# A graph convolution with a mixture of experts on one core: odd experts walk their chunks downwards, and the scaling stage is laid out anew

## The chip, the cores and the metric

The kernel runs on one core of a Trainium2 chip. The metric is the device time of one execution in microseconds (us). Engines are named as in the profile: PE is TensorE (PEld its weight loads), DVE is VectorE, ACT is ScalarE, POOL is GpSimd, SP is SyncE, which here only issues DMAs. L680 is line 680 of the kernel before.

## The reference

The input is `x` (12500 nodes of 256 features), 200000 edges `src`, `dst` (sorted by `dst`), a memory row `r`, and the weights of eight experts. Cut to what matters:

```python
h    = layernorm(x);  mems = h with row y replaced by r
near = the 7 rows of mems nearest to r          # squared distance
deg  = number of edges into a node (+7 for y) + 2;  dinv = 1 / sqrt(deg)
out[c] = sum over edges (s -> c) of dinv[s]*dinv[c]*(mems @ W)[s]  +  2*dinv[c]^2 * (mems @ W)[c]
x    = x + out
h    = layernorm(x)
e    = argmax(softmax(h @ gate_w + gate_b));  p = its probability
pos  = rank of the token among those of its expert; kept = pos < 1954
x    = x + p * kept * (relu(h @ w1[e] + b1[e]) @ w2[e] + b2[e])
```

## The kernel before

**Stage 1, to about 217 us.** The nodes lie in SBUF as 98 windows of 128 nodes (`nodes`), in seven chunks of 14 windows. POOL gathers 98 rows of sorted edges, one indirect DMA for each window (L665), in batches of seven; ACT counts in them (`count_first`, L761), which gives the degrees. Behind the count of each batch, ACT does ten squares (`far_square`, L766) of differences to `r` that DVE forms (`far_rows`, L1079, with `r_rows` in SBUF; a ring of 16 windows). When the degrees are known, each window is scaled in place by dinv and the layer norm: `scale_chunk`, chunks 1 and 6 on ACT (L772), the other five on DVE (L1208). SP stores each scaled chunk, in order from 0 to 6, into `z_table` in HBM (L535). ACT then clears `counts_f`, 6272 words in each partition (L794). PE turns the windows and ACT and DVE write them back as the start of the aggregate (L800, L1221).

**Stage 2, to about 1790 us.** POOL issues 1216 gathers of 128 rows from `z_table` (L680), after it has waited for the stores of all seven chunks. PE multiplies them with one-hot matrices (L1818), four gathers to a group; DVE adds the groups up. The ring holds four groups. Other edges are counted in `counts_f` and multiplied with pieces of `z_table` that SP loads. Convolution, second layer norm and gating run in the shadow of this. At the end `list_i` holds for each expert and place the row to fetch, and `taken_i` how many tokens each expert has.

**Stage 3, to the end.** An expert has room for 1954 tokens, eight chunks of 256 (`CHUNKS`, the last with 162). The 64 chunks are numbered n = 0 to 63, and s = n modulo 16 inside a pair of experts. All engines walk over all chunks, and a branch on the number of tokens taken skips the work on a chunk that starts beyond it; the semaphores of a skipped chunk are still counted up. PE does `up` (L2059), the transposes of the next chunk's rows (`turn_chunk`, L2041) and `down` (L2071). DVE copies the transposed rows (`feats`, L1638) and forms the results (`results`, L1670 to L1690). ACT normalizes the fetched rows of every chunk, skipped or not (`norm_rows`, L913), and does the bias and relu (L943).

POOL has no branch: it fetches and writes every chunk, skipped ones too (rows of a skipped chunk are written out of bounds, and so dropped).

```python
for n in range(FETCH):                 # FETCH = 6
    fetch(n)                           # two indirect DMAs, L729
for n in range(NE * NCH):
    if n + FETCH < NE * NCH:
        fetch(n + FETCH)
    for t in range(2):
        pool.wait_ge(S["res_ok"], 2 * n + t + 3)
        ... indirect DMA to out, L740
    if n % PC == PC - 1:               # the end of a pair of experts
        ... wait for the writes; sem_inc(S["pair_sent"], 1)
```

SP loads the weights of expert e + 2 (2 MB, L540, L541) when the results of expert e are through or skipped; there are two sets of weights.

Of the kernel before, what the change touches and what calls it, by code (L numbers as in the profile page):

```python
# [10 lines left out]
P = 128  # L11


def build(nc, x, src, dst, gnn_r, gnn_w, yidx, gate_w, gate_b, w1, b1, w2, b2, out):
# [79 lines left out]
    Z_ACT = (1, 6)  # L94
    Z_DVE = [c for c in range(NZC) if c not in Z_ACT]
    SQ_EACH, SQ_MID = 10, 4
    FAR_TO = [16, 30, 46, 60, 76, NW]
# [83 lines left out]
    PC = 2 * NCH  # L181
    XSLOTS = 8
    FB2 = FT // 2
    assert PC % XSLOTS == 0 and NCH % 2 == 0 and FB2 == 4 and KD == 2
# [3 lines left out]
    with ctx:  # L188
# [18 lines left out]
        count_up = bank[7][:, 0:P]  # L207
        strip_bank = [bank[2], bank[3]]
# [412 lines left out]
        def _(pool):  # L621
# [47 lines left out]

            for c in range(NZC):  # L670
                pool.wait_ge(chunk_moved[c], STORED[c])
# [49 lines left out]
            def fetch(n):  # L721

                slot = n % XSLOTS
                if n >= XSLOTS:
                    pool.wait_ge(S["res_ok"], 2 * (n - XSLOTS) + 4)
                    pool.wait_ge(S["xh_ok"], 2 * (n - XSLOTS) + 2)
                for t in range(2):
                    rows = list_i[:, 2 * n + t:2 * n + t + 1]
                    nc.gpsimd.indirect_dma_start(xs_rows[:, slot, t, :], None, x_rows,  # L729
                                                 bass.IndirectOffsetOnAxis(ap=rows, axis=0)).then_inc(S[f"xs_in{slot}"], 16)  # L730
# [3 lines left out]
            for n in range(NE * NCH):  # L734
                if n + FETCH < NE * NCH:
                    fetch(n + FETCH)
                for t in range(2):
                    m, slot = min(P, CHUNKS[n % NCH][1] - t * P), n % 2 * 2 + t
                    pool.wait_ge(S["res_ok"], 2 * n + t + 3)
                    nc.gpsimd.indirect_dma_start(  # L740
                        out, bass.IndirectOffsetOnAxis(ap=out_idx[0:m, 2 * n + t:2 * n + t + 1], axis=0), o_tile[0:m, slot, :], None,
                        bounds_check=last_node, oob_is_err=False).then_inc(S[f"out_done{slot}"], 16)
                if n % PC == PC - 1:
                    for slot in range(4):
                        pool.wait_ge(S[f"out_done{slot}"], 16 * (n + 1) // 2)
                    pool.sem_inc(S["pair_sent"], 1)
# [3 lines left out]
        def _(act):  # L750
# [40 lines left out]
            scale_chunk(Z_ACT[1])  # L791

            act.wait_ge(S["less_ok"], NW)
            nc.scalar.activation(counts_f, zeros[:, 0:1].to_broadcast([P, P * NW // 2]), ACT.Copy).then_inc(S["counts_clear"], 1)  # L794
# [128 lines left out]
            for q in range(NE // 2):  # L923
# [7 lines left out]
                for j in range(2):  # L931
                    for c in range(NCH):
                        n, s = CHUNKS[c][1], j * NCH + c
# [5 lines left out]
                        with act.If(all_took[q * 2 + j] > CHUNKS[c][0]):  # L939
                            act.wait_ge(S["l2_ps"], q * (2 * PC) + (2 * s + 2))  # L940
                            for f in range(FT):
                                act.wait_ge(S["l1_ps"], q * (PC * FB2) + ((s + 2) * FB2 + f // 2 + 1))
                                nc.scalar.activation(hid[:, f, 0:n], up_bank[f // 2][:, f % 2 * CR:f % 2 * CR + n], ACT.Relu,  # L943
                                                     bias=b1_pair[:, j * FT + f:j * FT + f + 1]).then_inc(S["hid_ok"], 1)
# [6 lines left out]
        def _(dve):  # L951
# [122 lines left out]
            def far_rows(first, last):  # L1074

                for w in range(first, last):
                    if w >= FR:
                        dve.wait_ge(S["square_ok"], w - FR + 1)
                    nc.vector.scalar_tensor_tensor(diff[:, w % FR, :, :], nodes[:, :, w, :], rstd[:, w:w + 1],  # L1079
                                                   r_rows[:, :].rearrange("p (k c) -> p k c", k=KD),  # L1080
                                                   ALU.mult, ALU.subtract).then_inc(S["diff_ok"], 1)
# [59 lines left out]

            far_rows(0, FAR_TO[0])
# [69 lines left out]
            for c in Z_DVE:  # L1212
                if c == Z_DVE[-1]:
                    far_rows(FAR_TO[4], FAR_TO[5])
                scale_chunk(c)

# [44 lines left out]

            dve.wait_ge(S["count_up_ps"], 1)
# [369 lines left out]
            def feats(q, s, took):  # L1632

                n = CHUNKS[s % NCH][1]
                with dve.If(took > CHUNKS[s % NCH][0]):
# [18 lines left out]
            def results(q, s, took):  # L1654

                j, c = s // NCH, s % NCH
                with dve.If(took > CHUNKS[c][0]):
                    for t in range(2):
                        n, slot = min(P, CHUNKS[c][1] - t * P), s % 2 * 2 + t
# [62 lines left out]
        def _(pe):  # L1722
# [28 lines left out]
            pe.wait_ge(S["row_id"], 3)  # L1751
            nc.tensor.matmul(count_up, ident[:, :], iota_r[:, :], start=True, stop=True).then_inc(S["count_up_ps"], 1)
# [280 lines left out]
            def turn_chunk(q, s):  # L2033

                n = CHUNKS[s % NCH][1]
# [13 lines left out]
            def up(q, s):  # L2049
                j, n = s // NCH, CHUNKS[s % NCH][1]  # L2050
                pe.wait_ge(S["xT_ok"], q * PC + (s + 3))
                if s % NCH == 0:
# [10 lines left out]
            def down(q, s):  # L2063
                j, n = s // NCH, CHUNKS[s % NCH][1]
# [16 lines left out]
            def turn_or_skip(q, s, took):  # L2081
                with pe.If(took > CHUNKS[s % NCH][0]):
# [5 lines left out]
            for q in range(NE // 2):  # L2088
                took = all_took[2 * q:2 * q + 3]
                for s in range(PC):  # L2090
                    inside = s % NCH < NCH - 1
                    with pe.If(took[s // NCH] > CHUNKS[s % NCH][0]):
# [4 lines left out]
                    with pe.Else():  # L2097
# [3 lines left out]
                        if inside:  # L2101
                            skip_turn(q, s + 1)
                    if not inside:
# [23 lines left out]
```

## Time and profile before

| | |
|---|---|
| median of 3 runs | 2517.27 us (2515.47 to 2517.34) |
| profiled execution | 2514.71 us, its span 2513.2 us |
| granted PE clock, mean | 0.894 of full speed |
| busy | PE 1964.8, POOL 1513.9, DVE 1313.4, ACT 1009.5 us |
| stage 1, to the first gather of stage 2 | 216.7 us |
| stage 2, to the first fetch of stage 3 | 1571.9 us |
| stage 3, to the end of the span | 724.6 us |

The span is what the profiler saw of one execution; 1.5 us lie around it. A busy share is a mean over stages with different limits, so the stages are read one by one.

### The profile page before, as it was taken

How to read it: one execution, taken by the hardware profiler on the slowest of the kernel's cores; microseconds unless marked ns; L12 is line 12 of the kernel's file. 1: busy time of each engine (PE TensorE's matmuls, PEld its weight loads, DVE VectorE, ACT ScalarE, POOL GpSimd, SP SyncE). 2: the span in 40 equal slices, each digit the busy share in tenths (PEclk: the TensorE clock that was granted, in tenths of full speed). 3: DMA queues.
4: the chain of work that ended last, by engine and by line, in shares of the span. 5: the costliest groups of instructions: out<-in, count | busy, mean ns of one | idle time of the engine just before them, and what ended most of it. 6: DMA issues, size and time to landing. Idle time of an engine off the chain costs nothing. (4 is left out here: it accounts for less than half of the span.)

```text
span 2513.2 us, 36856 instructions
## 1 busy us (share of the span) xinstructions
PE 1964.8 (78%) x11102; PEld 1697.2 (68%) x11102; DVE 1313.4 (52%) x3826; ACT 1009.5 (40%) x1897; POOL 1513.9 (60%) x1612
## 2 busy tenths in 40 slices
PE   3016778866876786887878889998699999999995
PEld 2005556755765675775767789887588788788874
DVE  7987874455245335345152358877444444445443
ACT  1577654355435435435253234342233323232332
POOL 6734777777777777777777777774223523422234
PEclk8557889988998998998989889999699999999998
DMA  9236335733663573663747779787313212212211
GB/s 264 76 107 202 106 105 181 236 105 105 208 209 105 180 235 106 200 215 117 258 147 235 219 209 240 217 233 178 93 37 73 85 34 75 74 39 69 62 49 29
DMA packets 235523, 359.07 MB, mean 143 GB/s; under 512 B 46584, under 2 KB 172696, under 8 KB 235220
## 3 DMA queue, kind: packets, MB, share of 16 engines
q0 software_dynamic: 74176, 194.10, 26.8%
q1 hardware_dynamic: 159860, 160.86, 21.0%
q10 hardware_dynamic: 1312, 2.10, 0.3%
q8 instruction: 71, 1.16, 0.2%
q14 instruction: 104, 0.85, 0.1%
HBM read 305.38 MB, written 56.40 MB: 144 GB/s over the span
## 5 line engine op out<-in xcount | busy, mean ns | idle before, releaser
L680 POOL DMA_INDIRECT arena<-z_table,arena x1216 | 1150.3, 946 | 434.4 <-issue 360.1
L1818 PE MATMUL bank<-arena 128*128 128x128 f32 x4864 | 708.8, 307 | 239.1 <-DMA arena<-z_table,arena 121.0
L1818 PEld LDWEIGHTS bank<-arena 128*128 128x128 f32 x4864 | 660.3, 217 | 333.6 <-issue 252.9
L1276 DVE TENSOR_TENSOR nodes<-nodes,bank 128x256 f32 x304 | 127.7, 420 | 696.1 <-PE bank L1818 676.5
L740 POOL DMA_INDIRECT out<-arena x128 | 130.2, 1017 | 410.8 <-DVE arena L1690 388.3
L2059 PE MATMUL bank<-arena 128*128 128x256 f32 (+1 forms) x1472 | 329.0, 383 | 9.1 <-DVE arena L1638 9.1
L943 ACT ACTIVATE nodes<-bank,arena 128x256 f32<-128x256 f32 (+1 forms) x368 | 152.4, 465 | 451.6 <-PE bank L2059 451.6
L2071 PE MATMUL bank<-arena,nodes 128*128 128x256 f32 (+1 forms) x1472 | 326.0, 379 | 0.0
L2059 PEld LDWEIGHTS bank<-arena 128*128 128x128 f32 x1472 | 281.8, 195 | 49.9 <-DVE arena L1638 11.7
L827 ACT ACTIVATE arena<-iota_h,arena 128x490 f16<-128x490 f16 x280 | 194.7, 695 | 290.2 <-PE bank L1830 290.0
L2071 PEld LDWEIGHTS bank<-arena,nodes 128*128 128x128 f32 (+1 forms) x1472 | 272.6, 187 | 40.1 <-issue 1.0
L1840 PE MATMUL bank<-arena,columns 128*128 128x256 f32 x1176 | 273.2, 383 | 3.5 <-ACT columns L817 3.5
L817 ACT ACTIVATE columns<-arena 128x768 f32<-128x768 uint16 (+3 forms) x102 | 153.1, 1506 | 262.3 <-PE bank L1840 259.2
L1840 PEld LDWEIGHTS bank<-arena,columns 128*128 128x128 f32 x1176 | 218.9, 193 | 30.3 <-issue 4.1
L1266 DVE TENSOR_TENSOR arena<-bank,arena 128x512 f32<-128x512 f32 x304 | 207.1, 682 | 0.2 <-DVE near L1231 0.2
L829 ACT ACTIVATE arena<-arena,ones 128x490 bf16<-128x490 f16 x280 | 196.9, 703 | 9.2
L729 POOL DMA_INDIRECT arena<-x_rows,list_i x128 | 124.8, 975 | 101.0 <-DVEq L1629 51.5
L1296 DVE TENSOR_TENSOR arena<-arena,bank 128x490 f32 x280 | 183.0, 654 | 0.5 <-issue 0.2
L1638 DVE COPY arena<-bank 128x512 f32<-128x512 f32 (+1 forms) x46 | 31.2, 678 | 211.4 <-PE bank L2041 204.8
L1830 PE MATMUL bank<-arena 128*128 128x490 bf16 x352 | 116.9, 422 | 23.5 <-DVE arena L1296 13.2
L665 POOL DMA_INDIRECT arena<-dst_rows,first_i x98 | 102.4, 1045 | 42.7 <-issue 29.3
L1670 DVE TENSOR_TENSOR arena<-bank,arena 128x256 f32<-128x256 f32 x92 | 38.9, 423 | 146.6 <-PE bank L2071 144.2
(321 smaller groups left out, 1881.3 us busy)
## 6 DMA issues: line engine op xcount, KB each, us to landing
arena<-z_table SPq DMA_DIRECT2D x96, 768.0 KB, 4.7
arena<-z_table,arena POOLq DMA_INDIRECT x1216
arena<-in_L_ffn_w SPq DMA_DIRECT2D x14, 1024.0 KB, 8.8
z_table<-nodes SPq DMA_DIRECT2D x14, 896.0 KB, 9.3
x_rows<-nodes SPq DMA_DIRECT2D x98, 128.0 KB
arena<-in_x SPq DMA_DIRECT2D x48, 256.0 KB, 3.1
out<-nodes SPq DMA_DIRECT2D x96, 128.0 KB
nodes<-in_x SPq DMA_DIRECT2D x12, 896.0 KB, 11.6
```

The lines of the kernel that those rows point to most:

```text
L680: nc.gpsimd.indirect_dma_start(gath[:, slot, t, :], None, z_table, bass.IndirectOffsetOnAxis(ap=src_idx[:, tile_at:tile_at + 1], axis=0)). ...
L740: nc.gpsimd.indirect_dma_start(out, bass.IndirectOffsetOnAxis(ap=out_idx[0:m, 2 * n + t:2 * n + t + 1], axis=0), o_tile[0:m, slot, :], Non ...
L817: nc.scalar.activation(count_f[:, j, 0:m, 0:nodes_in], counts[:, 0:nodes_in, c * HB:c * HB + m].rearrange("p n h -> p h n"), ACT.Copy).the ...
L827: nc.scalar.activation(far, iota_h[:, :], ACT.Abs, bias=neg_key[:, n:n + 1]).then_inc(S["key_ok"], 1)
L829: nc.scalar.activation(oh_key[:, n % 2, t, :], far, ACT.Relu, bias=ones[:, 0:1], scale=-1.0).then_inc(S["key_ok"], 1)
L943: nc.scalar.activation(hid[:, f, 0:n], up_bank[f // 2][:, f % 2 * CR:f % 2 * CR + n], ACT.Relu, bias=b1_pair[:, j * FT + f:j * FT + f + 1] ...
L1266: nc.vector.tensor_tensor(sel[:, step % SR, :, :], count_up.unsqueeze(1).to_broadcast([P, GT, P]), rel_b[:, t0:t0 + GT].unsqueeze(2).to_br ...
L1296: nc.vector.tensor_tensor(where, where, strip_bank[n % 2][:, 0:PW], ALU.add).then_inc(S["strip_added"], 1)
L1818: last = nc.tensor.matmul(agg_bank[i % AB][:, k * P:(k + 1) * P], gath[:, i, t, k * P:(k + 1) * P], sel[:, i, t, :], start=(t == 0), stop= ...
L1840: last = nc.tensor.matmul(piece_bank[:, 0:D], count_f[:, j, i, :], z_ring[:, j, i, :], start=False, stop=False)
L2059: last = nc.tensor.matmul(up_bank[b][:, i * CR:i * CR + n], w1_sb[:, j, k, f * P:(f + 1) * P], xs_feat[:, s % 2, k, 0:n], start=(k == 0), ...
L2071: last = nc.tensor.matmul(bank[4 + t][0:m, 0:D], hid[:, f, t * P:t * P + m], w2_sb[:, j, f, :], start=(f == 0), stop=(f == FT - 1))
```

## The change

In stage 3 an odd expert walks its chunks from the last to the first (`chunk_of`). POOL picks the columns of `list_i` to match, PE waits for the weights at each chunk of an odd expert and branches anew on the next chunk when it skips one. In stage 1, `far_rows` reads `r` from PSUM, where a matmul with the identity puts it; ACT scales chunks 1, 5 and 6; the last 22 windows of `far_rows` are spread between the chunks that DVE scales; `counts_f` is cleared by POOL, as soon as the degrees are final, instead of by ACT behind its last chunk.

```diff
-    Z_ACT = (1, 6)
+    Z_ACT = (1, 5, 6)
-    FAR_TO = [16, 30, 46, 60, 76, NW]
+    FAR_TO = [16, 30, 46, 60, 76, 84, 92, NW]
...
+    def chunk_of(s):
+        return CHUNKS[s % NCH] if s // NCH % 2 == 0 else CHUNKS[NCH - 1 - s % NCH]
...
+        r_bank = bank[7][:, P:P + D].rearrange("p (k c) -> p k c", k=KD)
...
(POOL, before the waits for the stores of the seven chunks)
+            pool.wait_ge(S["less_ok"], NW)
+            pool.wait_ge(S["deg_ok"], 2)
+            nc.gpsimd.memset(counts_f, 0.0).then_inc(S["counts_clear"], 1)
...
(POOL, fetch)
-                    rows = list_i[:, 2 * n + t:2 * n + t + 1]
+                    column = n // NCH * CT + chunk_of(n)[0] // P + t
+                    rows = list_i[:, column:column + 1]
...
(ACT)
-            scale_chunk(Z_ACT[1])
-
-            act.wait_ge(S["less_ok"], NW)
-            nc.scalar.activation(counts_f, zeros[:, 0:1].to_broadcast([P, P * NW // 2]), ACT.Copy).then_inc(S["counts_clear"], 1)
+            for c in Z_ACT[1:]:
+                scale_chunk(c)
...
(ACT; the same in feats, results, turn_chunk, up, down and their branches)
-                        n, s = CHUNKS[c][1], j * NCH + c
+                        n, s = chunk_of(j * NCH + c)[1], j * NCH + c
-                        with act.If(all_took[q * 2 + j] > CHUNKS[c][0]):
+                        with act.If(all_took[q * 2 + j] > chunk_of(s)[0]):
...
(DVE, far_rows)
-                                                   r_rows[:, :].rearrange("p (k c) -> p k c", k=KD),
+                                                   r_bank,
...
(DVE; the wait stood before the first select)
+            dve.wait_ge(S["count_up_ps"], 1)
             far_rows(0, FAR_TO[0])
...
-            for c in Z_DVE:
-                if c == Z_DVE[-1]:
-                    far_rows(FAR_TO[4], FAR_TO[5])
+            for i, c in enumerate(Z_DVE):
                 scale_chunk(c)
+                if i + 5 < len(FAR_TO):
+                    far_rows(FAR_TO[i + 4], FAR_TO[i + 5])
...
(PE)
+            pe.wait_ge(S["r_in"], 16)
+            nc.tensor.matmul(bank[7][:, P:P + D], ident[:, :], r_rows[:, :], start=True, stop=True)
...
-                if s % NCH == 0:
+                if s % NCH == 0 or j:
                     pe.wait_ge(S[f"w_in{j}"], q * 32 + 32)
...
-                        if inside:
+                        if inside and s < NCH:
                             skip_turn(q, s + 1)
+                        elif inside:
+                            turn_or_skip(q, s + 1, took[1])
```

## Rows read from the trace of the kernel before

**Rows 1.** The page: the span and three of its costliest groups.

```profile
span 2513.2 us, 36856 instructions
...
L680 POOL DMA_INDIRECT arena<-z_table,arena x1216 | 1150.3, 946 | 434.4 <-issue 360.1
...
L1266 DVE TENSOR_TENSOR arena<-bank,arena 128x512 f32<-128x512 f32 x304 | 207.1, 682 | 0.2 <-DVE near L1231 0.2
...
L1638 DVE COPY arena<-bank 128x512 f32<-128x512 f32 (+1 forms) x46 | 31.2, 678 | 211.4 <-PE bank L2041 204.8
```

**Rows 2.** Timeline of POOL, its first gather: start, us, instruction, idle time before it.

```profile
216.67 0.94 POOL L680 DMA_INDIRECT arena<-z_table,arena  x1 [64.25 <-DMA z_table<-nodes]
```

**Rows 3.** Windows, the stretch of the stores: PEclk, DMA share, GB/s come last.

```profile
170.00:215.00 45.00, 11.56 (x72) 10.76 (x71) 32.62 (x92) 36.18 (x103) 0.00 (x0) 0.54 1.00 283
```

**Rows 4.** Timeline, 163 to 206 us: SP's stores, DVE's and ACT's scaling, ACT's clearing.

```profile
168.66 40.91 SPq L535 DMA_DIRECT2D z_table<-nodes  x14
...
163.97 6.99 ACT L772 ACTIVATE nodes<-nodes,columns 128x256 f32<-128x256 f32 x14 [2.62 <-DVEq L1203]
...
200.34 5.41 ACT L794 ACTIVATE arena<-zeros 128x6272 f32<-128x6272 f32 x1
...
164.03 18.17 DVE L1208 TENSOR_SCALAR nodes<-nodes,columns 128x256 f32<-128x256 f32 x56 [0.15 <-DVE columns L1202]
```

**Rows 5.** Timeline of ACT: the first counts of batches 7 and 13.

```profile
96.77 0.40 ACT L761 ACTIVATE arena<-arena,columns 128x128 f32<-128x128 f32 x1 [4.24 <-DMA arena<-dst_rows,first_i]
...
154.27 0.40 ACT L761 ACTIVATE arena<-arena,columns 128x128 f32<-128x128 f32 x1 [1.72 <-DMA arena<-dst_rows,first_i]
```

**Rows 6.** Timeline of DVE and POOL at 24 us.

```profile
24.08 1.89 DVE L993 SCALAR_TENSOR_TENSOR arena<-arena 128x1664 f32<-128x1664 f32 x1
...
24.42 2.37 POOL L665 DMA_INDIRECT arena<-dst_rows,first_i  x1 [0.30 <-issue]
```

**Rows 7.** Groups of POOL by form: its longest memset.

```profile
L635 POOL MEMSET zeros<- 128x258 f32 x1 | 0.3, 308 | 0.0
```

**Rows 8.** Timeline of PE in stage 3, around four changes of expert.

```profile
1877.90 7.07 PE L2071 MATMUL bank<-arena,nodes 128*128 128x256 f32 x32
...
1899.31 1.03 PE L2071 MATMUL bank<-arena,nodes 128*128 128x256 f32 x4
...
1941.63 7.07 PE L2071 MATMUL bank<-arena,nodes 128*128 128x256 f32 x32
...
1964.47 7.07 PE L2071 MATMUL bank<-arena,nodes 128*128 128x256 f32 x32
...
2061.78 7.19 PE L2071 MATMUL bank<-arena,nodes 128*128 128x256 f32 x32
...
2077.78 7.07 PE L2071 MATMUL bank<-arena,nodes 128*128 128x256 f32 x32
...
2426.92 7.07 PE L2071 MATMUL bank<-arena,nodes 128*128 128x256 f32 x32
2438.66 1.09 PE L2041 MATMUL bank<-ident,arena 128*128 128x128 f32 x4 [4.67 <-DVEq L1642]
...
2451.13 7.07 PE L2071 MATMUL bank<-arena,nodes 128*128 128x256 f32 x32
```

**Rows 9.** Timeline of POOL behind the last chunk of expert 0 that is not skipped.

```profile
1891.20 0.97 POOL L729 DMA_INDIRECT arena<-x_rows,list_i  x1 [0.30 <-issue]
...
1896.40 0.97 POOL L729 DMA_INDIRECT arena<-x_rows,list_i  x1 [0.31 <-issue]
```

**Rows 10.** The fetches (L729): time from issue to landing.

```profile
DMA to landing us min/median/max: 2.7/3.0/7.1
```

**Rows 11.** The writes (L740): the same.

```profile
DMA to landing us min/median/max: 2.1/2.5/7.7
```

**Rows 12.** Chain that ended last: POOL's writes behind the last result, first and last of 11.

```profile
2489.89 0.98 POOL out L740
...
2502.78 1.09 POOL out L740
```

More of the change, by code:

```diff
@@ L181, in build @@
     PC = 2 * NCH
+    def chunk_of(s):
+        return CHUNKS[s % NCH] if s // NCH % 2 == 0 else CHUNKS[NCH - 1 - s % NCH]
     XSLOTS = 8
     FB2 = FT // 2
-    assert PC % XSLOTS == 0 and NCH % 2 == 0 and FB2 == 4 and KD == 2
+    assert CT == 2 * NCH and PC % XSLOTS == 0 and NCH % 2 == 0 and FB2 == 4 and KD == 2
     ARENA = 20096
@@ L737, in _ @@
                 for t in range(2):
-                    m, slot = min(P, CHUNKS[n % NCH][1] - t * P), n % 2 * 2 + t
+                    m, slot = min(P, chunk_of(n)[1] - t * P), n % 2 * 2 + t
                     pool.wait_ge(S["res_ok"], 2 * n + t + 3)
@@ L1259, in near_chosen @@
                 dve.sem_inc(S["chosen_ok"], 1)
-            dve.wait_ge(S["count_up_ps"], 1)
             def select(step):
@@ L1632, in feats @@
             def feats(q, s, took):
-                n = CHUNKS[s % NCH][1]
-                with dve.If(took > CHUNKS[s % NCH][0]):
+                n = chunk_of(s)[1]
+                with dve.If(took > chunk_of(s)[0]):
                     dve.wait_ge(S["xT_ps"], q * PC + (s + 2))
@@ L1654, in results @@
             def results(q, s, took):
-                j, c = s // NCH, s % NCH
-                with dve.If(took > CHUNKS[c][0]):
+                j = s // NCH
+                with dve.If(took > chunk_of(s)[0]):
                     for t in range(2):
-                        n, slot = min(P, CHUNKS[c][1] - t * P), s % 2 * 2 + t
+                        n, slot = min(P, chunk_of(s)[1] - t * P), s % 2 * 2 + t
                         token = xs_rows[0:n, s % XSLOTS, t, :]
@@ L2033, in turn_chunk @@
             def turn_chunk(q, s):
-                n = CHUNKS[s % NCH][1]
+                n = chunk_of(s)[1]
                 pe.wait_ge(S["xh_ok"], q * (2 * PC) + (2 * s + 2))
@@ L2049, in up @@
             def up(q, s):
-                j, n = s // NCH, CHUNKS[s % NCH][1]
+                j, n = s // NCH, chunk_of(s)[1]
                 pe.wait_ge(S["xT_ok"], q * PC + (s + 3))
-                if s % NCH == 0:
+                if s % NCH == 0 or j:
                     pe.wait_ge(S[f"w_in{j}"], q * 32 + 32)
@@ L2063, in down @@
             def down(q, s):
-                j, n = s // NCH, CHUNKS[s % NCH][1]
+                j, n = s // NCH, chunk_of(s)[1]
                 for t in range(2):
@@ L2081, in turn_or_skip @@
             def turn_or_skip(q, s, took):
-                with pe.If(took > CHUNKS[s % NCH][0]):
+                with pe.If(took > chunk_of(s)[0]):
                     turn_chunk(q, s)
@@ L2091, in _ @@
                     inside = s % NCH < NCH - 1
-                    with pe.If(took[s // NCH] > CHUNKS[s % NCH][0]):
+                    with pe.If(took[s // NCH] > chunk_of(s)[0]):
                         up(q, s)
```

## The prediction

> **What bounds the kernel now.** I read the page first, then the timeline of POOL, then windows over the stretch of the stores, then the timeline of PE in stage 3, and last the chain that ended last.
>
> Stage 2 is POOL's. L680 has 1216 gathers of 0.946 us and 0.30 us of issue behind each; of its 434.4 us of idle time 360.1 are that issue, and most of the rest is the one wait of 64.25 us before the first gather [rows 1, 2]. So POOL issues a gather each 1.25 us without a break, 1520 us in all, and what PE, DVE and ACT do in that time counts only if they fall four groups behind. The first gather waits for the stores of the seven chunks [rows 2]. From 170 to 215 us the DMA engines are busy all the time, at 283 GB/s [rows 3]. So the first gather comes 48.0 us after the first store (216.67 - 168.66), and the first store comes as soon as DVE has scaled chunk 0 [rows 2, 4]. Only what moves the end of chunk 0 moves stages 1 and 2.
>
> What makes the degrees late? ACT counts a batch each 9.58 us ((154.27 - 96.77) / 6) and waits for the gathers before each [rows 5]. ACT's own work on a batch is shorter, or it would not wait. Seven gathers at the undisturbed 1.246 us take 8.72 us [rows 1], so 0.86 us per batch and 5.2 us over the six are lost. The trace shows how: a gather that POOL begins at 24.42, under a DVE instruction with two inputs in SBUF, takes 2.37 us and not 0.94; DVE's instruction ends at 25.97, and 0.82 us later the gather is through [rows 6]. It was held until DVE was done. `far_rows` has two SBUF inputs too and runs through these batches.
>
> Stage 3 is PE's. From one `down` to the next are 14.25 us while chunks follow each other inside an expert. By PE's groups the experts have 6, 4, 8, 5, 8, 8, 4 and 3 chunks that are not skipped, 46 in all, as the count of L1638 says [rows 1]. At a change of expert the time between the two `down` is 21.41 us behind expert 0 (two skipped), 22.84 behind expert 1 (four), 16.00 behind expert 2 (none), and 24.21 behind expert 6 (four) [rows 8]. Behind the last result, POOL still issues 11 writes, ten of them for the five skipped chunks of expert 7 [rows 12].
>
> **The change, part by part.** `r` in PSUM. `far_rows` has one SBUF input then. L1266 reads one input from PSUM, runs 304 times beside the gathers of stage 2, and their mean stays at 0.946 us [rows 1]. So of the 5.2 us, those that `far_rows` causes fall away; DVE's short limit computations between them keep their two SBUF inputs. I take 4.0 us off the time of the first store (bounds 0 and 5.2). The extra matmul and the earlier wait for it lie far ahead of `far_rows`, where PE idles. The Trainium skill says otherwise of one step: its page "SBUF — State Buffer", section "Who interferes with whom", lets a DVE instruction with two SBUF inputs hold up only GpSimd instructions that read SBUF, and infers that descriptor generation needs the write interface; by that the change would take off nothing here and the sum would be 4.0 us higher. The rows speak against it [rows 6].
>
> Chunk 5 to ACT. ACT's last chunk ended at 200.34, and a third chunk adds 6.99 us [rows 4]: chunk 5 would be ready at 200.3 and chunk 6 at 207.3 at worst. The stores want them 5 and 6 times 6.86 us after 168.66, at 203.0 and 209.8. Hidden. DVE has one chunk less, and its last 22 `far_rows` only change places. Both cost nothing as long as the DMA engines have a chunk to store; if chunk 6 were late, each us would delay the gathers by one.
>
> Clearing by POOL. It takes 5.41 us from ACT [rows 4]. That lets the turning of the windows begin earlier, but PE only gets ready sooner for gathers that POOL issues at its own pace: 0. On POOL it lies where POOL waits for the stores anyway. Its length: 258 words take 0.308 us [rows 7], so between 5.4 (ACT's time for the same shape) and 7.5 us (by proportion). But POOL starts it with the very semaphore that starts DVE on chunk 0, at 164.03 [rows 4]. DVE's 56 windows take 18.17 us, 0.325 us each, so chunk 0 takes 4.6. A DVE instruction can keep POOL out to its very end [rows 6]. If they do it in the other too, DVE stands still for the length of the clearing before chunk 0 is done, and the first store is 5.4 us late. Bounds 0 and 7.5 us; I take 5.3, near the upper end, since the one overlap that the rows show was an exclusion to the end of the instruction. The stages 1 and 2 then come out at -4.0 + 5.3 = +1.3 us.
>
> The same section of that page of the Trainium skill states such an exclusion, in both directions and by who issues first, for DVE's 2-port modes, which tensor_scalar can enter; by it the clearing costs its full length here, the 5.3 us taken above. No row of this trace shows DVE held by POOL.
>
> The order of chunks. Skipped chunks now lie together in the middle of each pair: runs of 6, 3, 0 and 9, and none between pairs. Behind expert 2 there is now the run of three that lay behind expert 3, and behind expert 3 a direct change: these two swap. Behind expert 1 the change becomes direct, 16.00 in place of 22.84: -6.8 us. Left are the runs of 6 and 9.
>
> A fetch runs only six chunks ahead, in POOL's queue, and POOL does four DMAs for each chunk, skipped or not. The fetch of the first chunk behind a run of 6 is issued right behind the last writes of the last real chunk; behind a run of 9, three rounds later. In the trace, the fetch at that place in the queue (chunk n = 12, behind the real n = 5) starts its second DMA at 1891.20, which is 13.3 us after the last `down` (1877.90) [rows 8, 9]. A round is 1896.40 - 1891.20 = 5.20 us. Before, that chunk was one of the skipped ones behind expert 1's four real ones; now it is the next real one.
>
> - Run of 9 (before expert 7): second DMA at 13.3 + 3 x 5.2 = 28.9 us, landed 3.0 us later [rows 10], two activations of `norm_rows` 1.1 us, transposes at 33.0. From transposes to `down` are 12.5 us (2451.13 - 2438.66) [rows 8], in which the first `up` takes 10.07 us where others take 7.07: the granted clock has fallen in the pause. 45.5 us in place of 24.2: +21.3 us.
> - Run of 6 (before expert 1): second DMA at 13.3, landed after 3.0 to 7.1 us [rows 10], since SP loads 2 MB of weights at that time; I take 5.1. Transposes at 19.5, `down` at 32.0, in place of 21.4: +10.6 us (8.5 to 12.6).
>
> Is DVE's walk through the skips later than that? Four skips cost 24.21 and two 21.41, 1.4 us each, so 6 come to 27.0 and 9 to 31.2: sooner than POOL in both. POOL is behind with its writes after a run, and DVE's results wait for a free `o_tile`; I find that below 3 us, beside 7 us of `up`. Weights are loaded an expert ahead as before.
>
> The end. One write instead of 11 behind the last result: 2502.78 - 2489.89 = 12.9 us less [rows 12]. But the last write is a real one, 2.5 us to landing in place of 2.1, at most 7.7 [rows 11]: I take 12.2 (7.3 to 12.5).
>
> Sum of stage 3: -6.8 + 21.3 + 10.6 - 12.2 = +12.9 us. All: +14.2 us. The profiled execution would go from 2514.7 to 2528.9 us; it lies 2.6 us below the median of the runs, so the median goes from 2517.3 to 2531.5 us.
>
> **The rivals.**
>
> - B, the clearing doesn't hold DVE: POOL gets the port only when `far_rows` runs behind chunk 0, or a write on its own takes nothing from DVE. For it: no row shows DVE held. Then -4.0 + 12.9 = +8.9 us, 2526.2 us.
> - C, the late fetches are hidden, faster: if the fetches behind a run come soon enough, a run costs only DVE's walk, 27.0 and 31.2: 5.6 + 7.0 - 6.8 - 12.2 = -6.4 us. With +1.3 from stage 1 that is 2512.2 us, with -4.0 it is 2506.9. It decides at the place where the fetch of chunk 61 lands: at 17 us behind the start of the last `down` or sooner (31.2 - 12.5 - 1.1) it is C. Against it: the code puts that fetch behind three rounds of four DMAs, and a round takes 5.20 us [rows 9].
> - D, more than the sum: the pile of POOL's work behind the run of 6 reaches DVE and through it PE, or the rows that land late in the weights' load cost 7 us more, or chunk 6 is late for its store. One more stall of 7 us on PE: 2538.5 us.
> - E, `r` in PSUM does nothing: sum without the 4.0, 2535.5 us.
>
> **How the numbers follow.** My forecast 0.45, B 0.27, C 0.10, D 0.08, E 0.10. About 0.2%, 5 us, is what a measurement of this kernel can tell from no change. The forecast, B, D and E are slower by more, though B comes near: with a shorter landing and the full 5.2 us of stage 1 it is +5.5. C splits into faster (-10) and just at the edge (-5). Slower 0.84, same 0.08, faster 0.08. The range takes in B and E with the bounds of landing and of the clearing: 2522 to 2538 us.
>
> **What would show it.** The PE's gap before expert 7 some 45 us from `down` to `down`, before expert 1 some 32, POOL's L729 without a break in both, and PE's transposes waiting for ACT; 16 us behind experts 1 and 3; one write behind the last result; L665 near 0.95 us from 97 us on; the first window of chunk 0 on DVE or its neighbour longer by 5 us beside POOL's memset, and the first store at about 170 us (B: 165). I am wrong if POOL fetches earlier than its queue says, or if a gap before an expert is under 30 us behind the run of nine.

## The result, and the profile after

The changed kernel takes 2526.71 us (median of 6 runs, 2526.43 to 2528.88), the kernel before, measured beside it, 2517.31 us (6 runs, 2515.47 to 2519.12). The ratio is 1.0041 with a 95% interval of 1.003 to 1.0051: 9.4 us slower. The forecast was 2531.5 us with a range of 2522 to 2538. The profiled execution took 2526.62 us, 11.9 us more than that of before, where the sum had said 14.2. The mean granted clock is 0.894 in both. Of all runs in this document one was slow (2630.07 us at a mean granted clock of 0.791, an execution of experiment 3), and it is in none of the figures.

Rows of the page of the changed kernel, which answer to [rows 1]. The 1216 gathers of stage 2 take what they took; the gathers of stage 1 stand below them, and the last line is theirs on the page of before.

```profile
span 2525.1 us, 36883 instructions
...
L688 POOL DMA_INDIRECT arena<-z_table,arena x1216 | 1150.5, 946 | 423.1 <-issue 360.1
...
L670 POOL DMA_INDIRECT arena<-dst_rows,first_i x98 | 98.1, 1001 | 43.0 <-issue 29.3
...
L665 POOL DMA_INDIRECT arena<-dst_rows,first_i x98 | 102.4, 1045 | 42.7 <-issue 29.3
```

**Stages 1 and 2.** Timeline of the changed kernel, 160 to 219 us: start, duration, instruction, and in brackets the idle time before it with what ended it. First DVE, then POOL, then ACT, then SP's stores. The first line is of a view of DVE cut off at 161 us, which shows the first window of chunk 0 by itself.

```profile
160.07 5.50 DVE L1217 TENSOR_SCALAR nodes<-nodes,columns 128x256 f32<-128x256 f32 x1 [0.15 <-DVE columns L1211]
...
160.07 9.69 DVE L1217 TENSOR_SCALAR nodes<-nodes,columns 128x256 f32<-128x256 f32 x14 [0.15 <-DVE columns L1211]
...
172.83 4.59 DVE L1217 TENSOR_SCALAR nodes<-nodes,columns 128x256 f32<-128x256 f32 x14
...
160.10 5.33 POOL L677 MEMSET arena<- 128x6272 f32 x1 [11.62 <-DVEq L1212]
218.44 0.95 POOL L688 DMA_INDIRECT arena<-z_table,arena  x1 [53.00 <-DMA z_table<-nodes]
...
188.46 13.84 ACT L781 ACTIVATE nodes<-nodes,columns 128x256 f32<-128x256 f32 x28
...
169.80 40.94 SPq L540 DMA_DIRECT2D z_table<-nodes  x14
```

The degrees are ready at 160.07 us and not at 164.03 [rows 4]: 3.96 us sooner. DVE's chunk 0 then takes 9.69 us where the next chunk of the same 14 instructions takes 4.59, and beside it lies POOL's clearing of 5.33 us. The whole loss is in the first of the 14 windows: it takes 5.50 us (the median of these instructions is 0.396) and ends at 165.57, the clearing at 165.43. So the first store comes at 169.80, 1.14 us later than before. The first gather comes at 218.44, 1.77 us later than before [rows 2]; 0.60 us of that are added behind the stores: 7.70 us from the end of SP's stores to the first gather (218.44 - 169.80 - 40.94), and before 7.10 (216.67 - 168.66 - 40.91) [rows 2, 4]. The extra time is in the DMA engines and not in POOL. Windows over the end of the stores in the changed kernel:

```profile
214.00:216.00 2.00, 2.00 (x20) 2.00 (x19) 1.95 (x5) 1.74 (x6) 0.00 (x0) 1.00 1.01 287
...
216.25:217.25 1.00, 1.00 (x12) 1.00 (x11) 0.98 (x3) 0.84 (x4) 0.00 (x0) 1.00 0.07 22
217.25:218.25 1.00, 1.00 (x12) 1.00 (x10) 0.98 (x3) 0.90 (x3) 0.00 (x0) 1.00 0.00 0
```

The engines are full to about 216.2 us, then their mean share is 0.07 for another 1.0 us, about what one busy engine of sixteen would give, and POOL's gather comes 1.2 us after the last of it. Before, the same views have the engines full to 215.1, all bytes moved by 215.5, and the gather again 1.2 us later. ACT's chunks 5 and 6 end at 202.30, and the stores follow each other as before. PE's first `down` is at 1808.66, 1.59 us later than before.

**Stage 3.** Timeline of PE in the changed kernel, the changes of expert behind experts 0, 1, 2 and 3, and behind expert 6.

```profile
1879.48 7.07 PE L2080 MATMUL bank<-arena,nodes 128*128 128x256 f32 x32
1901.39 1.11 PE L2050 MATMUL bank<-ident,arena 128*128 128x128 f32 x4 [14.84 <-ACT arena L921]
1903.29 8.88 PE L2068 MATMUL bank<-arena 128*128 128x256 f32 x32 [0.78 <-DVE arena L1645]
...
1912.44 7.07 PE L2080 MATMUL bank<-arena,nodes 128*128 128x256 f32 x32
...
1954.76 7.07 PE L2080 MATMUL bank<-arena,nodes 128*128 128x256 f32 x32
...
1970.50 7.07 PE L2080 MATMUL bank<-arena,nodes 128*128 128x256 f32 x32
...
2067.81 7.19 PE L2080 MATMUL bank<-arena,nodes 128*128 128x256 f32 x32
...
2146.75 7.07 PE L2080 MATMUL bank<-arena,nodes 128*128 128x256 f32 x32
...
2162.49 7.07 PE L2080 MATMUL bank<-arena,nodes 128*128 128x256 f32 x32
...
2431.10 7.07 PE L2080 MATMUL bank<-arena,nodes 128*128 128x256 f32 x32
2464.78 1.11 PE L2050 MATMUL bank<-ident,arena 128*128 128x128 f32 x4 [26.61 <-ACT arena L921]
2466.68 8.78 PE L2068 MATMUL bank<-arena 128*128 128x256 f32 x32 [0.78 <-DVE arena L1645]
...
2475.74 7.07 PE L2080 MATMUL bank<-arena,nodes 128*128 128x256 f32 x32
```

Before expert 1 PE waits 14.84 us for ACT's `norm_rows`, before expert 7 26.61 us, and `up` behind such a pause takes 8.8 us and not 7.07. Windows over that `up` of expert 7 and the pause ahead of it (busy us of PE, PEld, DVE, ACT and POOL, then PEclk, DMA share, GB/s) show why: the granted clock is 0.50, the level of 1.2 GHz, in 16 us in which PE works for 1.11 us, 0.60 on average in the first five us around the start of `up`, and 1.00, the level of 2.4 GHz, in the next.

```profile
2450.00:2466.00 16.00, 1.11 (x4) 0.71 (x4) 0.06 (x1) 3.27 (x6) 12.34 (x13) 0.50 0.32 57
2466.00:2471.00 5.00, 4.32 (x13) 3.56 (x14) 0.63 (x1) 1.43 (x4) 3.78 (x5) 0.60 0.17 44
2471.00:2476.00 5.00, 5.00 (x27) 4.41 (x26) 0.06 (x1) 2.55 (x8) 3.78 (x5) 1.00 0.21 52
```

From `down` to `down` (before: [rows 8], and 23.61 us behind expert 3, read in the same view): 32.96 us where it was 21.41, 15.74 where it was 22.84, 22.37 and 15.74 where it was 16.00 and 23.61, 44.64 where it was 24.21.

Timeline of POOL in the changed kernel, between the last real chunk of expert 6 and the first of expert 7. L738 are fetches, L749 writes.

```profile
2441.81 1.00 POOL L749 DMA_INDIRECT out<-arena  x1 [2.44 <-ACT arena L921]
2443.11 0.99 POOL L738 DMA_INDIRECT arena<-x_rows,list_i  x1 [0.30 <-issue]
...
2452.21 1.00 POOL L749 DMA_INDIRECT out<-arena  x1 [0.30 <-issue]
2453.52 0.99 POOL L738 DMA_INDIRECT arena<-x_rows,list_i  x1 [0.31 <-issue]
...
2457.41 1.00 POOL L749 DMA_INDIRECT out<-arena  x1 [0.30 <-issue]
2458.72 0.99 POOL L738 DMA_INDIRECT arena<-x_rows,list_i  x1 [0.31 <-issue]
2460.01 0.97 POOL L738 DMA_INDIRECT arena<-x_rows,list_i  x1 [0.30 <-issue]
```

The first real chunk of expert 7 is fetched in the fourth pair of L738, at 2458.72 and 2460.01. The second is 28.9 us behind the start of the last `down` (2431.10), to the tenth what the prediction had. POOL never waits in between; each round costs it 5.2 us.

ACT's `norm_rows` of the first real chunk of expert 1 and of expert 7, and the landing times of L738 over the whole kernel (its own view):

```profile
1900.24 1.09 ACT L921 ACTIVATE arena<-arena 128x256 f32<-128x256 f32 x2 [7.83 <-DMA arena<-x_rows,list_i]
...
2463.64 1.09 ACT L921 ACTIVATE arena<-arena 128x256 f32<-128x256 f32 x2 [3.62 <-DMA arena<-x_rows,list_i]
...
DMA to landing us min/median/max: 2.7/3.0/7.4
```

What ends PE's wait is ACT, and what ends ACT's wait is the landing of the rows. For expert 7 ACT begins 3.6 us after the second fetch was issued (2460.01), for expert 1 7.4 us after it (1892.79): there the DMA share is 0.98 at 331 GB/s between 1895 and 1901 us.

The end, timeline of POOL in the changed kernel:

```profile
2511.05 0.98 POOL L749 DMA_INDIRECT out<-arena  x1 [9.38 <-DVE arena L1697]
2514.50 0.98 POOL L749 DMA_INDIRECT out<-arena  x1 [2.47 <-DVE arena L1697]
```

One write is left behind the last result, where there were 11 [rows 12]. From the start of the last `down` to the end of the span are 21.3 us (2525.1 - 2503.8), before 34.0 (2513.2 - 2479.2). So the 11.9 us of the profile are +1.6 up to the first `down`, +23.0 from the first to the last, and -12.7 behind it.

### The profile page after: what moved, and what is told of

It reads as the page before. It is cut to its first block and busy times, and to the rows that moved or that the text cites. A ratio compares the mean times of both kernels' runs of the same rounds, so it can differ in the third digit from the quotient of the medians.

```text
span 2525.1 us, 36883 instructions
## 1 busy us (share of the span) xinstructions
PE 1961.8 (78%) x11104; PEld 1693.4 (67%) x11104; DVE 1311.8 (52%) x3812; ACT 1012.7 (40%) x1910; POOL 1515.9 (60%) x1613
## 5 line engine op out<-in xcount | busy, mean ns | idle before, releaser
L749 POOL DMA_INDIRECT out<-arena x128 | 130.7, 1021 | 414.9 <-DVE arena L1697 390.9
L738 POOL DMA_INDIRECT arena<-x_rows,list_i x128 | 125.1, 978 | 105.7 <-issue 54.2
L1645 DVE COPY arena<-bank 128x512 f32<-128x512 f32 (+1 forms) x46 | 31.2, 679 | 251.1 <-PE bank L2050 248.9
L1839 PE MATMUL bank<-arena 128*128 128x490 bf16 x352 | 118.3, 428 | 17.7 <-DVE arena L1303 10.6
L1291 DVE TENSOR_SCALAR arena<-bank,arena 128x128 bf16<-128x128 f32 x352 | 114.4, 342 | 0.0
```

The costliest lines, as they stand in the source:

```text
L749: nc.gpsimd.indirect_dma_start(out, bass.IndirectOffsetOnAxis(ap=out_idx[0:m, 2 * n + t:2 * n + t + 1], axis=0), o_tile[0:m, slot, :], Non ...
```

## The experiments

"Changed" is the changed kernel: 9.4 us above before in its own runs, and 11.1 us in a second set with three of the experiments (forecast 9 to 11). The chips differ between sets, so a time is compared by its distance to before on its own chip, and differences of 1 to 2 us between sets tell nothing.

**1. The order of chunks alone.** The kernel before with `chunk_of`, POOL's columns and PE's branches as changed. The matmul that puts `r` into PSUM and the earlier wait are in it, but nobody reads it.

```diff
+    def chunk_of(s):
+        return CHUNKS[s % NCH] if s // NCH % 2 == 0 else CHUNKS[NCH - 1 - s % NCH]
...
-                    rows = list_i[:, 2 * n + t:2 * n + t + 1]
+                    column = n // NCH * CT + chunk_of(n)[0] // P + t
+                    rows = list_i[:, column:column + 1]
```

> The kernel before with the new order of chunks alone (r is still read from SBUF, ACT scales two chunks and clears the counts). If stage 3 pays for the order and nothing else does, the two long gaps of PE come out as in the changed kernel (33 us from down to down before expert 1, 44.6 us before expert 7) and the time is 10 to 12 us above the kernel before, that is 0 to 1.5 us below the changed kernel. If the loss had come from stage 1 (the rival), this kernel would be within 2 us of the kernel before.

Measured: 2528.29 us, 11.8 us above before (ratio 1.0047, 1.003 to 1.0063). The two long gaps are 32.84 and 44.79 us. From the first `down` to the last are 695.2 us (before 672.1), behind it 21.4 (before 34.0): stage 3 costs +10.4 us, in its own execution, and the changed kernel's +10.3. The order is where the loss comes from. The time is within the 10 to 12 us that were expected above before, but it isn't below the changed kernel's 9.4. Stage 1 was expected to be as in before, and its degrees were ready only at 166.69 us, 2.66 later, and its first gather came at 219.05, 2.38 later. That is 0.6 us behind the changed kernel; the rest of the distance lies in stage 2 (53.34 us from its last gather to the first fetch, 51.20 in the changed kernel; see experiment 4). DVE and POOL in stage 1 of this kernel show why the degrees are late, and the last line is the held gather in the kernel before:

```profile
97.27 6.42 DVE L1086 SCALAR_TENSOR_TENSOR arena<-nodes,columns,r_rows 128x256 f32<-128x256 f32 x16
...
98.36 1.00 POOL L670 DMA_INDIRECT arena<-dst_rows,first_i  x1 [0.30 <-issue]
99.67 4.84 POOL L670 DMA_INDIRECT arena<-dst_rows,first_i  x1 [0.31 <-issue]
...
102.37 2.07 POOL L665 DMA_INDIRECT arena<-dst_rows,first_i  x1 [0.31 <-issue]
```

One gather, begun at 99.67 while DVE runs 16 instructions with two SBUF inputs back to back, is through at 104.51: 0.82 us after the last of the sixteen ended (97.27 + 6.42 = 103.69). The gather before it took 1.00 us under the same instructions. In the kernel before, two gathers under such a stretch take 1.22 and 1.27 us, and the third, begun at 102.37, is through at 104.44, again 0.82 us after the last of the sixteen (103.62). So the stretch lets gathers through until one is caught, and what it costs is decided by how early that is.

All of this is in one batch of seven gathers. From the start of the batch begun at 95.5 to 95.9 us to the start of the next are 8.83 us in the changed kernel, 10.46 before, 12.96 in this kernel and 11.54 in that of experiment 4. The four batches behind it take 35.3 us in the changed kernel and 37.6 us in each of the three others: there no gather takes over 1.3 us, but many take 1.1 to 1.3. About 2.3 us of the loss come back in every kernel with `r` in SBUF, and 1.6 to 4.1 depend on the catch.

**2. The new stage 1 alone.** Every expert walks upwards again.

```diff
-        return CHUNKS[s % NCH] if s // NCH % 2 == 0 else CHUNKS[NCH - 1 - s % NCH]
+        return CHUNKS[s % NCH]
```

> The changed kernel with every expert walking its chunks upwards again: the new stage 1 alone. Expected: first store at 169.8 us, first gather 1 to 2 us later than before, the gaps of PE between experts as before (21.4, 22.8, 16.0, 24.2 us), 11 writes behind the last result, and a time 0 to 2 us above the kernel before. If stage 1 costs the larger part, it is 8 us or more above.

Measured: 2518.51 us, 2.0 us above before (1.0007, 0.9997 to 1.0016). First store at 169.98, first gather at 218.63, 1.96 us later than before. The gaps are 21.29, 24.67, 16.01, 22.33 and 23.83 us. As expected: stage 1 costs about 2 us, and cannot be told from nothing by the time alone. The gap behind expert 1 is 1.8 us longer than before and the one behind expert 3 1.3 shorter, in code that is the same.

**3. The clearing after the store of chunk 3**, and again with the changed kernel on one chip.

```diff
-            nc.gpsimd.memset(counts_f, 0.0).then_inc(S["counts_clear"], 1)
             for c in range(NZC):
                 pool.wait_ge(chunk_moved[c], STORED[c])
+                if c == 3:
+                    nc.gpsimd.memset(counts_f, 0.0).then_inc(S["counts_clear"], 1)
```

> The changed kernel with POOL clearing the counts after the store of chunk 3 has landed, and not when the degrees are ready. My theory (the clearing holds DVE in chunk 0): DVE's chunk 0 takes 4.6 us again and not 9.7, the first store comes at 164.7 us and not 169.8, the first gather 5 us sooner, and the time falls by 5 us against the changed kernel. The rival (chunk 0 is long because DVE and ACT begin to scale together, or because of the columns): chunk 0 stays near 9.7 us and the time is unchanged. A third case: chunk 0 is early, but the DMA engines or POOL's later clearing give it back, and the first gather moves by less than 2 us.

> The changed kernel itself, on the same chip as the next three, so that they can be compared with it directly: 2526 to 2528 us, 9 to 11 us above the kernel before.

> The late clearing a second time: at its first run its profiled execution was 4.6 us shorter than that of the changed kernel, but its median only 1 to 3 us lower. My theory (the 5.05 us by which the first gather came sooner pass through to the end): 4 to 5 us below the changed kernel in the median of the same chip too. The rival (something later gives 2 to 3 us back): 2 us.

Timeline of the first of the two, DVE, SP and POOL:

```profile
159.94 4.62 DVE L1218 TENSOR_SCALAR nodes<-nodes,columns 128x256 f32<-128x256 f32 x14 [0.15 <-DVE columns L1212]
...
164.58 40.92 SPq L540 DMA_DIRECT2D z_table<-nodes  x14
...
192.16 5.33 POOL L680 MEMSET arena<- 128x6272 f32 x1 [43.81 <-DMA z_table<-nodes]
213.39 0.95 POOL L689 DMA_INDIRECT arena<-z_table,arena  x1 [15.89 <-DMA z_table<-nodes]
```

Chunk 0 takes 4.62 us again, the first store comes at 164.58 and the first gather at 213.39: 5.2 and 5.05 us sooner than in the changed kernel. The times: 2524.53 us at first (8.0 above before, 1.003, 1.0019 to 1.0041); then 2524.59 beside 2529.30 for the changed kernel on one chip (1.0027, 1.0018 to 1.0036, beside 1.0047, 1.0033 to 1.006), 4.7 us less. Across chips the first comparison shows 1.4 us (9.4 and 8.0); on one chip the gain is what the first gather had gained. The clearing held DVE; that rival B of the prediction is wrong is shown.

**4. `r` from SBUF again**, in the changed kernel; the matmul stays.

```diff
-                                                   r_bank,
+                                                   r_rows[:, :].rearrange("p (k c) -> p k c", k=KD),
```

> The changed kernel, but the differences read r from SBUF again (two SBUF inputs on DVE); the matmul that puts r into PSUM stays. My theory (such an instruction holds up POOL's gathers): POOL's first gathers take more than 2 us in places again, the degrees are ready at about 164.0 us and not 160.1, and the time rises by 4 us (3 to 5) against the changed kernel. Rival E (r in PSUM does nothing, the 4 us came from elsewhere): the degrees stay at 160.1 us and the time is unchanged. By the Trainium skill, page "SBUF — State Buffer", section "Who interferes with whom", it would be the second.

Measured: 2535.37 us (1.0073, 1.0056 to 1.0089), 9.4 us more above before than the changed kernel (18.8 and 9.4). POOL in it:

```profile
99.57 1.28 POOL L670 DMA_INDIRECT arena<-dst_rows,first_i  x1 [0.30 <-issue]
101.15 3.25 POOL L670 DMA_INDIRECT arena<-dst_rows,first_i  x1 [0.30 <-issue]
```

The degrees come at 165.21, the first gather at 223.58, both 5.14 us later than in the changed kernel. Rival E is wrong: with `r` in SBUF POOL's gathers are held, in the three kernels that read it there (degrees at 164.03, 165.21, 166.69), and with `r` in PSUM none of those from 97 us to the last at 147.5 us takes over 1.2 us in the changed kernel (degrees at 160.07, and within 0.4 us of it in the other kernels that read PSUM). The whole price was missed, though: 9.4 us where 3 to 5 were expected. In its profiled execution 3.6 us more pass between the last gather and the first fetch (54.76 and 51.20 us), in code that is the same. That stretch took between 51.1 and 54.8 us in all kernels, whatever they changed, and what decides it is open. The 5.14 us at the first gather are shown; the rest of the price is not explained.

**5. Fetches five, and seven chunks ahead** instead of six.

```diff
-    FETCH = 6
+    FETCH = 5        (e_fetch7: 7)
```

> The changed kernel with the fetches of token rows five chunks ahead and not six. My theory (behind a run of skipped chunks PE waits for a fetch that stands in POOL's queue behind one round of four DMAs for each skipped chunk beyond what the fetches lead by): one round of 5.2 us more in both long gaps, 38 us before expert 1 and 50 us before expert 7, and about 10 us more than the changed kernel (9 to 12; more if other changes of expert begin to wait as well). The rival (the gaps are the walk of the engines through the skipped chunks, or the weights): no change.

> The changed kernel with the fetches seven chunks ahead. My theory: one round of 5.2 us less in both long gaps (27 to 28 us before expert 1, where DVE's walk through six skipped chunks, 27 us, is next; 39.5 us before expert 7), so 10 us less than the changed kernel, if a fetch so far ahead does not wait for its slot (it needs the results of chunk n - 8, one chunk behind the last real one, so 5 to 10 us). The rival (walk or weights): no change.

Measured: 2538.52 us with five (1.0086, 1.0069 to 1.0102), 2519.32 us with seven (1.0011, 1.0001 to 1.0021), that is 22.3 and 3.1 us above before, where the changed kernel is 9.4 above. The gaps before expert 1 and before expert 7:

| fetches ahead | before expert 1 | before expert 7 |
|---|---|---|
| 5 | 37.26 us | 50.97 us |
| 6 (changed) | 32.96 us | 44.64 us |
| 7 | 27.53 us | 40.45 us |
| 11 | 28.40 us | 31.29 us |

One chunk of lead moves a gap by 4.2 to 6.3 us, about a round of POOL. The gaps with six are late fetches, not the walk and not the weights. The times moved less evenly: with five 12.9 us more than the changed kernel (9 to 12 expected), with seven 6.3 less (10 expected). With seven the two gaps together fell by 9.6 us, about what the theory asks for, but the stretch from the last gather to the first fetch took 54.78 us in the profiled execution and not 51.20. The last row is that of the next experiment.

**6. Fetches eleven chunks ahead, into twelve slots**, alone and with the late clearing. The slots lie in a free part of `nodes`; POOL waits for the stores of stage 2 (`out_x1`) ahead of its first fetch, and four semaphores that count one event each are merged with others.

```diff
-    FETCH = 6
+    FETCH = 11
-    XSLOTS = 8
+    XSLOTS = 12
...
-        xs_rows = carve([XSLOTS, 2, XW])
+        spare = nodes[:, :, :, :].rearrange("p k w c -> p (k w c)")[:, FT * CR:FT * CR + XSLOTS * 2 * XW]
+        xs_rows = spare.rearrange("p (s t c) -> p s t c", s=XSLOTS, t=2)
...
+            pool.wait_ge(S["out_x1"], OUT_ALL)
             for n in range(FETCH):
                 fetch(n)
-            pool.wait_ge(S["out_x1"], OUT_ALL)
```

> The changed kernel with the fetches eleven chunks ahead into twelve slots: no fetch behind a skipped run is late any more. My theory: what is left of the long gaps is the walk of DVE and ACT through the skipped chunks, 27 us before expert 1 and 31 us before expert 7 (from 33.0 and 44.6), so 19 us less than the changed kernel, about 2507 us, some 10 us below the kernel before. The rivals: the weights of the next expert or the writes that pile up behind a run are late as well, and the gaps stay above 35 us (gain under 10 us); or PE is faster than the walk says and the gaps fall towards 16 us.

> Both at once: fetches eleven chunks ahead into twelve slots, and the counts cleared after the store of chunk 3. The two act in different stages, so the gains should add: 19 + 5 = 24 us less than the changed kernel, about 2503 us, 14 us below the kernel before. If only one of the two theories holds, it is -19 or -5 us.

Measured: 2507.39 us (0.9965, 0.9953 to 0.9978) and 2502.48 us (0.9945, 0.9929 to 0.9962). The first is 8.8 us faster than before and the second 13.7, on one chip; against the changed kernel's 9.4 that is 18.2 and 23.1 us less, where 19 and 24 were expected. PE before expert 7 with the early fetches alone:

```profile
2427.56 7.07 PE L2081 MATMUL bank<-arena,nodes 128*128 128x256 f32 x32
2447.72 1.08 PE L2051 MATMUL bank<-ident,arena 128*128 128x128 f32 x4 [13.08 <-ACT arena L922]
...
2458.85 7.07 PE L2081 MATMUL bank<-arena,nodes 128*128 128x256 f32 x32
```

PE still waits for ACT, but 13.08 us and not 26.61. ACT no longer waits for a DMA there; its own view in this kernel says "issue", where it named the DMA of L738 in the changed kernel:

```profile
2435.11 4.04 ACT L922 ACTIVATE arena<-nodes 128x256 f32<-128x256 f32 x8 [4.56 <-issue]
...
2446.85 1.09 ACT L922 ACTIVATE arena<-nodes 128x256 f32<-128x256 f32 x2 [1.07 <-issue]
```

The gap of 31.29 us is the 31.2 that the prediction had worked out as the walk through nine skips (1.4 us each), and before expert 1 it is 28.40 where the walk was put at 27.0. The sum fits better than its parts: PE's transposes start 20.2 us after the last `down` and not 18.7, and from them to the next `down` are 11.1 us and not 12.5.

**7. The clearing by ACT again**, behind its last scaled chunk; all else as changed.

```diff
-            nc.gpsimd.memset(counts_f, 0.0).then_inc(S["counts_clear"], 1)
...
             for c in Z_ACT[1:]:
                 scale_chunk(c)
+            act.wait_ge(S["less_ok"], NW)
+            nc.scalar.activation(counts_f, zeros[:, 0:1].to_broadcast([P, P * NW // 2]), ACT.Copy).then_inc(S["counts_clear"], 1)
```

> The changed kernel with the counts cleared by ACT again, behind its last scaled chunk; all else (r in PSUM, three chunks by ACT, the order of chunks) stays as changed. My theory: the clearing costs nothing on ACT, so this is the late clearing's equal: first store at 164.7 us, and 4 to 5 us below the changed kernel. The rival (ACT is late with the turned windows, PE with its first groups, and POOL has to wait for a free slot): above the late clearing by up to the 5.4 us of ACT's instruction.

Measured: 2522.69 us (1.0017, 1.0008 to 1.0027), 6.6 us below the changed kernel on the same chip (4 to 5 expected) and 1.9 below the late clearing, which the intervals don't separate. Its ACT, SP and POOL:

```profile
198.41 5.42 ACT L800 ACTIVATE arena<-zeros 128x6272 f32<-128x6272 f32 x1
...
164.33 40.88 SPq L540 DMA_DIRECT2D z_table<-nodes  x14
...
212.00 0.95 POOL L685 DMA_INDIRECT arena<-z_table,arena  x1 [63.92 <-DMA z_table<-nodes]
```

The 5.42 us of ACT cost nothing, against the rival. The first gather comes 6.8 us after the end of SP's stores; with the clearing on POOL it was 7.7 (changed) and 7.9 to 8.5 (late). So the first gather is 1.8 us sooner than in the second late clearing (212.00 and 213.81). Windows of 0.2 us over the end of the stores show where that lies: in all fourteen profiles the gather comes 1.0 to 1.6 us after the last bytes of the stores. In the three profiles with the clearing on ACT the engines fall from full to idle within 0.2 to 0.4 us, in the eleven with the clearing on POOL a tail with a share under 0.5 lasts 1.0 to 1.6 us. So it is the stores that end late and not POOL that starts late; why a clearing on POOL, long over by then, gives the stores a tail is open.

**8. The old order with the early fetches and the late clearing**, the edit of experiment 2 on top of 6.

> The early fetches and the late clearing with every expert walking upwards, as before the change. It tells what the new order is worth once no fetch is late. My theory: the new order's runs then cost only the walk (its seven changes of expert sum to 144.5 us from down to down, the old ones to 140 us), and it saves 12.7 us of writes at the end, so the old order is slower by 8 us: about 2510 us. The rival (the old order gains from the early fetches too, as much or more): the two are within 2 us, and the new order is worth nothing.

Measured: 2510.95 us (0.9972, 0.9962 to 0.9981). Against the new order on the other chip that is 8.5 us more by the medians, 6.5 by the distances to before. In the profiles the new order loses 3.6 us from the first `down` to the last (676.8 and 673.1) and wins 12.8 behind it (19.1 and 31.9). So the new order is worth 6 to 9 us, but only once no fetch is late; 8 were expected.

## Why the prediction was right

- **`r` in PSUM, -4.0 us.** Measured -3.96 at the degrees. The mechanism is confirmed (experiment 4). That the size came out to 0.04 us is luck: it is what this one execution of before had lost. Two other kernels with `r` in SBUF lost 5.1 and 6.6 us, because their long catch (3.25 and 4.84 us) came earlier in the first stretch, and the upper bound of 5.2 was too low for the second. The prediction spread the loss evenly over six batches; in the trace of before 1.6 us of it are in one batch and 2.3 in the four behind it. By the Trainium skill, page "SBUF — State Buffer", section "Who interferes with whom", read as the prediction read it, none of this should occur for a DMA's descriptors; the traces disagree. That section of the Trainium skill does let GpSimd instructions that read SBUF be held, and these gathers take their row numbers from a tile in SBUF (`first_i`); whether it is that read which waits, no run tells.
- **The clearing holds DVE, +5.3 us.** Measured +5.10 (9.69 - 4.59) for a clearing of 5.33, and taken back by both ways of moving it (experiments 3 and 7). The same section of that page of the Trainium skill has the exclusion run in both directions for DVE's 2-port modes, and here the trace agrees in so far as DVE stood still; no run tells which mode DVE's windows were in. The Trainium skill gives the ports there to whoever issues first, and that isn't borne out by the recorded starts: DVE's window starts at 160.07, POOL's clearing at 160.10, and it is DVE that waits. What the sum lacked is 0.6 us behind the stores. Stages 1 and 2: +1.77 us at the first gather, forecast +1.3.
- **Chunk 5 to ACT: nothing.** ACT ended at 202.30 and the DMA engines had work throughout. Confirmed.
- **The fetches behind a run.** The place of the fetch, 28.9 us, was right. Before expert 1 the gap grew by 11.6 us (forecast 10.6), before expert 7 by 20.4 (forecast 21.3). Two errors offset each other in both. The rows came later than the sum had them: the transposes started 21.9 us after the last `down` and not 19.5 (the landing took 7.4 us, the forecast took 5.1 of 3.0 to 7.1), and 33.7 and not 33.0. And from the transposes to `down` passed 11.0 us and not 12.5, since `up` took 8.8 us and not 10.07: the granted clock was back at 1.00 about 3.3 us after the start of the `up` of expert 7, and in the kernel before about 5.9 us after it (estimates: windows of the changed kernel show 0.51 from 2468 to 2470 us and 1.00 from 2470 on, those of before 0.50 from 2441 to 2445 and 0.72 from 2445 to 2448). No run tells why sooner. Experiments 5 and 6 show the mechanism.
- **The direct change behind expert 1**: -7.1 us (forecast -6.8). **The swap behind experts 2 and 3**: -1.5 us, forecast 0; a run of three costs 22.37 us in the new place where it cost 23.61 in the old, and the direct change 15.74 where it was 16.00.
- **The end**: -12.7 us, forecast -12.2.

Stage 3 gave +10.3 us where the sum had +12.9. The 2.6 us are the swap (1.5), the long gap (0.9), the end (0.5), the direct change behind expert 1 (0.3) and 0.4 spread over the rest of the stage, less the 1.0 by which the run of six was dearer. The profiled executions differ by 11.9 us and the medians by 9.4: the profiled execution of before lay 2.6 us below its median, and the prediction carried that distance over to the changed kernel, whose profiled execution lies 0.1 below its own. So half of the miss of 4.8 us is in the terms and half in the step from the profile to the median. Rival C failed at the point that the prediction had named: the fetch was issued at 28.9 us and landed by 32.5, not at 17. Rival B's time, 2526.2 us, lies closer to the measured 2526.71 than the forecast does, so the time alone would have spoken for B. What rules it out is DVE's window of 5.50 us and experiments 3 and 7.

## What to carry to other kernels

A reordering that gathers empty work into one run turns a prefetch that is deep enough on average into one that is late: count the lead in the queue's own rounds at the longest run, and deepen it first (here six chunks to eleven turned +9 us into -9). A "free" instruction on an idle engine is not free if it starts on the same semaphore as the work on the critical path; put it behind a later event, or leave it where it cost nothing (here on ACT). Read gathers one by one: a mean of 1.07 us over 98 hid one of 4.84, and under it a slower pace of all batches that came back in every such kernel. And when the time comes out right, look whether a rival's time is as near: here the rows had to decide.

## What the hardware showed that was not expected

- Back-to-back DVE instructions with two SBUF inputs kept one indirect DMA's issue on POOL out until 0.82 us after the last of sixteen had ended (4.84 us), and let the one before it through in 1.00 us.
- POOL's clearing of 128x6272 fp32 took 5.33 us, ACT's 5.42; the proportion from the small one had said up to 7.5. It delayed one DVE tensor_scalar by 5.10 us (5.50 and not 0.40), nearly its whole length, and the 13 behind it not at all.
- With the clearing on POOL, even one that had ended at 165 us, the stores had a tail of 1.0 to 1.6 us at a low DMA share and the first gather came 7.7 to 8.5 us behind the end of SP's stores, with the clearing on ACT 6.8 to 7.1 and a tail of 0.2 to 0.4. No run tells why.
